# Value-product groups of an attention step at units 7 and 10 of their own step and 0 and 3 of the next

## What is computed

```python
q = x @ Wq.T
k = x @ Wk.T * scale
v = x @ Wv.T
qk = jnp.einsum('bthd,bshd->bhts', qh, kh)
causal = jnp.tril(jnp.ones((S, S), dtype=bool))
qk = jnp.where(causal, qk, -jnp.inf)
attn = jax.nn.softmax(qk, axis=-1)
qkv = jnp.einsum('bsdh,bhts->bthd', vh, attn)
...
return ln @ Wo.T
```

## Time and profile before

| | us |
|---|---|
| median of 3 runs | 651.88 |
| the profiled execution, whole | 650.15 |
| its span, first to last instruction | 648.4 |
| attention steps in it | about 51 to 398 |
| expert part in it | about 400 to 648 |

### The profile page before, as it was taken

The page is one execution under the profiler, slowest core; times in us unless marked ns, Lnnn a source line. Parts: engine busy times, 40 slices in busy tenths (PEclk is TensorE's granted clock), DMA queues, the critical chain, the costliest instruction groups (busy, mean ns, idle before and its releaser), DMA issues.

```text
span 648.4 us, 16200 instructions
## 1 busy us (share of the span) xinstructions
PE 570.3 (88%) x5145; PEld 413.1 (64%) x5146; DVE 465.3 (72%) x1592; ACT 402.5 (62%) x716; POOL 244.3 (38%) x328
## 2 busy tenths in 40 slices
PE   3679999899999999999999986999878999999940
PEld 1245555555555556455555543999877999999940
DVE  3788777688778778887887773687675666666636
ACT  3505777586777767876876776675644556565512
POOL 6201301032452533533614335355545333333326
PEclk9999999899999999999999999999999999999985
DMA  6544568535253253353252101112241211111138
GB/s 173 187 108 147 153 194 261 161 107 188 60 172 105 77 178 85 98 187 92 89 188 60 52 14 48 30 35 55 56 117 52 59 49 49 49 46 45 42 111 297
DMA packets 66117, 69.37 MB, mean 107 GB/s; under 512 B 9620, under 2 KB 57108, under 8 KB 66052
## 3 DMA queue, kind: packets, MB, share of 16 engines
q1 hardware_dynamic: 61156, 57.46, 30.4%
q0 software_dynamic: 4320, 8.99, 4.4%
q10 hardware_dynamic: 576, 2.10, 0.8%
HBM read 36.92 MB, written 31.03 MB: 105 GB/s over the span
## 4 chain that ended last, share of the span: by engine, by line
PE 58%; DMA 9%; DVE 9%; ACT 9%; issue 7%; POOL 3%; SPq 2%; another core or an unknown queue 1%; ACTq 0%; POOLq 0%; DVEq 0%
PE psN L759 16%; PE psO L541 8%; PE psO L770 8%; PE psN L507 5%; PE psT L522 5%; ACT probs L887 4%; DMA k_parts_dram<-kparts 3%; DMA kst_all<-k_parts_dram 3%; PE psT L524 3%; PE psN L509 3%; DVE negm L1134 2%; PE psM L567 1%; PE psM L549 1%; DMA qst_all<-mrow 1%; PE psM L571 1%
## 5 line engine op out<-in xcount | busy, mean ns | idle before, releaser
L1134 DVE TENSOR_REDUCE negm<-psN 128x1 f32<-128x512 f32 (+3 forms) x352 | 214.9, 635 | 59.2 <-PE psN L509 57.1
L887 ACT ACTIVATE probs<-psT 128x512 f32<-128x512 f32 x320 | 183.9, 596 | 67.2 <-PE psT L524 66.6
L759 PE MATMUL psN<-probs 128*128 128x128 f32 x1136 | 141.0, 277 | 2.9 <-ACT probs L1009 2.3
L759 PEld LDWEIGHTS psN<-probs 128*128 128x128 f32 x1136 | 134.2, 194 | 3.8 <-issue 3.6
L1759 POOL DMA_INDIRECT expert_out<-kst_all,dest x71 | 69.2, 975 | 112.2 <-DVE kst_all L1530 107.5
L522 PE MATMUL psT<-qst_all,kst_all 74*128 74x256 bf16 (+2 forms) x384 | 100.2, 279 | 11.0 <-ACT probs L887 8.3
L507 PE MATMUL psN<-kst_all,qst_all 74*128 74x256 bf16 (+2 forms) x384 | 103.1, 288 | 6.3 <-DMA kst_all<-k_parts_dram 5.2
L541 PE MATMUL psO<-probs,vaug 128*32 128x512 f32 (+3 forms) x1024 | 95.8, 447 | 0.3
L509 PE MATMUL psN<-kst_all,qst_all 117*128 117x128 bf16 x512 | 93.6, 228 | 0.0
L1009 ACT ACTIVATE probs<-gu_w 128x1024 f32 x71 | 74.9, 1056 | 23.8 <-PE psN L759 19.0
L1506 DVE TENSOR_TENSOR probs<-probs,psN 128x512 f32<-128x512 f32 x71 | 48.7, 685 | 53.8 <-PE psN L759 27.6
(11 more groups left out here) (235 smaller groups left out, 721.2 us busy)
## 6 DMA issues: line engine op xcount, KB each, us to landing
q_parts_dram<-qparts SPq DMA_DIRECT2D x24, 384.0 KB, 3.5
k_parts_dram<-kparts SPq DMA_DIRECT2D x24, 384.0 KB, 3.6
qst_all<-q_parts_dram SPq DMA_DIRECT2D x32, 288.0 KB
kst_all<-k_parts_dram SPq DMA_DIRECT2D x32, 288.0 KB
kst_all<-dispatched SPq DMA_DIRECT2D x71, 66.0 KB
xall<-in_x SPq DMA_DIRECT2D x8, 256.0 KB, 4.1
gu_w<-in_gateT SPq DMA_DIRECT2D x4, 512.0 KB, 5.0
gu_w<-in_upT SPq DMA_DIRECT2D x4, 512.0 KB, 5.7
```

What stands on the lines that cost most here:

```text
L759: mm = pe.matmul(bank[par][:, c * P:(c + 1) * P], ew[par][:, half, c * P:(c + 1) * P], xgT[par], start=True, stop=True)
L887: nc.scalar.activation(probs[:, g % 2, 512 * u:512 * (u + 1)], psT[:, u % TBANKS, :], ACT.Exp, scale=SOFTMAX_SCALE).then_inc(exp_done, 1)
L1134: nc.vector.tensor_reduce(dst, src, axis=AX.X, op=ALU.max, negate=True).then_inc(nat_done, 1)
```

## The change

On TensorE the groups move: group 0 from unit 9 to unit 7, group 1 from unit 1 of the next step to unit 10 of its own, group 2 from unit 3 to unit 0, group 3 from unit 5 to unit 3. On ScalarE the copy moves from unit 6 to unit 4 and `place_v` from unit 7 to unit 5. Behind the last step two groups instead of three are left over.

```diff
@@ TensorE, step @@
-                    if k in (1, 3, 5) and there(b, g, -1):
-                        values(*step_at(b, g, -1), (k + 1) // 2)
-                    if k == 9:
-                        values(b, g, 0)
+                    if k in (0, 3) and there(b, g, -1):
+                        values(*step_at(b, g, -1), 3 if k else 2)
+                    if k in (7, 10):
+                        values(b, g, int(k == 10))
...
-            for c in range(1, TB):
+            for c in range(2, TB):
                 values(L, 3, c)
@@ ScalarE, step @@
-                    if k == 6 and there(b, g, -1):
+                    if k == 4 and there(b, g, -1):
                         keep_values(*step_at(b, g, -1))
-                    if g == 0 and k == 7 and has_earlier(b):
+                    if g == 0 and k == 5 and has_earlier(b):
                         place_v(b)
```

## The result

The changed kernel takes 663.76 us (median of 6 runs, 659.39 to 669.43), the kernel before beside it 651.67 us (6 runs, 650.87 to 654.55). The ratio is 1.0166, with a 95% interval from 1.0129 to 1.0202. (Ratios here leave out single disturbed runs, medians don't, so the two differ a little.) The forecast was 655.5, with a range up to 660.5: the direction was right, the size three times too small.

The account below looks back on a forecast made before the run. In-order TensorE, busy 43.23 of 45 us in steady attention, bounds the kernel; only its standstills can change. +1.0 us a batch over seven batches, +7.0, less 3.4, gives +3.6: 655.5 us on the 651.88 median, range 645.5 to 660.5.

Parts of the forecast that it names:

- the mechanism in g = 0: Step g = 0: copy ahead of `mrow` delays it, so TensorE idles 0.85 us before L571; +0.4 us a batch.
- g = 1: Step g = 1: value projection's wait for `mrow`, about +0.3 us, paid back by 0.29 at unit 9; taken as 0.
- the waits at unit 7 of g = 2 and g = 3: TensorE would wait 0.5 to 1 us before unit 7's scores in these steps, and not before unit 8's.
- +1.0 a batch: Sum over the four steps of a batch, +0.4 + 0 + 0.7 - 0.15 with rounding; range +0.5 to +1.4 us.
- +0.7: Step g = 2: units 4 to 7 lose their value group, so TensorE stands still; range +0.3 to +0.9 us.
- late news: TensorE's semaphores reach other engines up to 1.5 us late around GpSimd's scatters; basis of a slower rival, chance 0.18.
- V1 ahead of the step's first unit: Group 1 at unit 10 fills waits at step starts: the load at 115.05 and three g = 2 starts; -3.4 us.
- zero at the tail: Last batch: last `mrow` 0.5 us later, last V0 out of the way 1 us sooner; net effect taken as zero.
- +7.0: The +1.0 us a batch taken over seven batches, before the 3.4 us of filled waits is subtracted.
- the faster case: Rival: ScalarE's gates do not close, waits go, perhaps the clock stays up; 643 to 648 us, chance 0.27.
- the heavier rival: Slower by more: exponential 0 of g = 3 held behind GpSimd's scatter, +0.7 a batch, +5; 660 us, chance 0.18.
- The load chain as pacemaker: Rival, no change: casts and DMAs from key projection to g = 2's stacks and maxima set every batch; 652 us, chance 0.10.

Follow-up runs that it names:

- mrow_first: Changed kernel with `mrow` copied ahead of `oT` on ScalarE in g = 0, 1 and 3: 643.35 us, ratio to before 1.0168.
- first pair: The first two profiles: the kernel before, profiled execution 650.15 us, and the changed kernel as it is, profiled execution 659.39 us.
- second: Second pair of profiles, on one chip: the kernel before (profiled run 646.65 us) and the changed kernel as it is (median 662.8 us).
- after_third: Changed kernel as it is, run again on a chip where before takes 650.2 us: 662.8 us, ratio to before 1.0225.
- last_batch_old: Changed kernel with the old places kept in the last batch's four steps: 644.61 us against 633.56 for before, ratio 1.0188.
- after_again: Changed kernel as it is, run again on a chip where before takes 631.9 us: 645.8 us, ratio to before 1.0239.
- groups_sooner: Kernel before with groups 1, 2, 3 at units 0, 1, 3 of the next step, copy left at 6: 660.6 us, ratio 1.0143.
- copy_sooner: Kernel before with groups 1, 2, 3 at units 0, 1, 3 of the next step, copy at 4, group 0 at 9: 664.3 us, ratio 1.0200.
- spread_evenly: Kernel before with groups 0 and 1 at units 8 and 10, 2 and 3 at next step's 2 and 5, copy at 6: 662.1 us, ratio 1.0194.

## Why the prediction was right in direction and wrong in size

- **Right: the mechanism in g = 0.** `mrow` 0.47 behind the copy, as forecast, and an idle TensorE ahead of L571, 0.69 instead of 0.85. `mrow_first` shows that 0.48 us a batch hang on it.
- **Right: g = 1**, at 0, and the waits at unit 7 of g = 2 and g = 3, of 0.41 and 0.52.
- **Right, in part by luck: +1.0 a batch.** Batches 2 to 6 lose 4.1 us in the first pair of profiles and 4.7 in the second, 0.8 to 0.9 each. Step by step, as in the table above, g = 2 loses a little more than its +0.7, at or past the end of its range, and g = 3 less or more by chip. In g = 0 the +0.43 of the first pair is luck: three batches lose 0.1 on average, and two lose 0.9, in which exponential 1 starts 1.4 us behind its scores; on the faster chip each loses 0.25. In g = 3 exponential 1 comes 1.56 to 1.61 us behind the step's start (forecast 1.55 to 2.3), and the next batch starts 9.11 behind it (forecast 9.1). But late news moves these parts: exponential 1 of g = 3 comes 2.2 us behind the step's start in four batches of `after_third`. On a faster chip the batch loses 1.4 us.
- **Wrong: "V1 ahead of the step's first unit", -3.4 us.** This is the term that failed first. In the changed kernel the wait near 115 did not shrink in any profile: 2.08, 2.10 and 2.29 us against 1.99 and 2.03. TensorE stood ready at 113.1 in both kernels of the first pair, since batch 1 had lost V1's time before, 0.65 of it at L571. The three waits at starts of g = 2 steps went from 0.59, 0.82 and 0.85 to 0, 0.58 and 0.41, so 1.3 of the 2.5 us came. (The 0.82 was misread besides: the profile names the DMA of `mrow` there, not the stacks, and V1 fills it only in part.) Alone V1's move measured +8.4. I priced only what V1 fills, and not what it covered at unit 1; with both counted, a batch loses 1 us, as shown above.
- **Wrong: zero at the tail.** The last batch lost 3.2 us in the first pair and 1.6 in the second (39.2 against 37.7). I took "the last `mrow` is 0.5 later" as hidden. In the first pair half clock lay on top. `last_batch_old` shows that 0.8 us of it hang on the new places in the g = 2 step; the rest of it no run takes apart.
- **So the sum:** batches 0 to 6 lost 6.7 us in the first pair, against +7.0, with the half clock of batch 1 and the lucky start of batch 0 in them. The credit of 3.4 did not come on top, and the tail added 3.2. These two make up the distance in the profiles, 9.2 against 3.6. The medians lie 12.1 apart; the changed kernel's profile is of its fastest run of six.
- **Wrong by what was left out: the clock.** I made its fall a term only of the faster case. In the first pair it went the other way: 6.8 us at half clock instead of 3.4 in batch 1, and one fall in batch 7. A single pair doesn't settle that: in the second it was before that had 6.8 us in batch 1, and the changed kernel 3.4. The mean clocks of all runs speak for more falls in the changed kernel, worth at most 3 to 4 us. The Trainium skill ("TensorE: Matmul & The Clock Gate", What's actually happening) has an idle array fall to half clock; the rows agree in that filling the wait at 113 kept the clock at 1.00, but the length of the wait alone did not decide: after 2.29 us in `after_again` it stayed up.
- **The rivals.** Faster did not come: new waits opened at unit 7. Late news at exponential 0 of g = 3, as the heavier rival had it, did not come in the changed kernel; the scores of unit 0 end at 264.67 and their exponential starts at 264.71, beside the next scatter:

```profile
264.45 0.22 PE L524 MATMUL psT<-qst_all,kst_all 117*128 117x128 bf16 x1
...
264.71 0.60 ACT L887 ACTIVATE probs<-psT 128x512 f32<-128x512 f32 x1 [0.24 <-PE psT L524]
264.75 0.95 POOL L1674 DMA_INDIRECT dispatched<-rows,slots  x1 [1.51 <-ACT probs L887]
```

It came one unit later, at exponential 1, in `after_third`, at exponential 1 of g = 0 in two batches of the first pair, and at exponential 0 in `groups_sooner`, `copy_sooner` and `spread_evenly`. But the changed kernel loses 2.4% on a faster chip, where it is as good as absent, so it is not what makes the change slow. The load chain as pacemaker holds in one place, batch 5: in kernels with before's order the stacks came at the same time, 291.6 to 291.9, whether TensorE was early or not.

What stays open is why nearly every other place for the groups costs about 1 us a batch. Each order shows other waits, part of V1's cost has no row, and the parts that were tried on slower chips alone carry late news.

## What to carry to other kernels

When a block of work moves within an in-order engine, price two things: what it fills where it goes, and what it hid where it was. The second is found by asking of each wait right behind the old place which engine would be late if this one came sooner by the block's length. And count standstills on TensorE twice, once for themselves, once for the chance that the clock falls behind them.

## What the runs showed of the hardware

**Chips differ.** The kernel before takes 632 to 634 us on two chips and 650 to 652 on the others, with the same program and inputs. On the slower ones TensorE's semaphores reach the others late around GpSimd's scatters: counted over the attention part, some 60 to 90 matmuls of a trace have their semaphore over 0.25 us behind their end. On the faster ones there are 0 to 6. I had this effect in a rival, but not that it belongs to the chip.

**The first step can run at half clock with the page showing 1.00.** The key projection near 55 us takes twice as long in some executions of either kernel. The first row is of before, where the clock's record begins only at 58.1, the second of the changed kernel:

```profile
55.27 2.03 PE L571 MATMUL psM<-hT,wk 128*128 128x512 f32 x2
```

```profile
54.21 1.12 PE L571 MATMUL psM<-hT,wk 128*128 128x512 f32 x2
```

In the second pair it was before that had the fast start and after the slow one: batch 0 took 40.1 and 43.9 us, which is chance and no part of the change.
